# A fused graph network: the first attention chunk moved from the second norm into the first gate step

## What is computed

```python
x = _layernorm(x + _L0_gnn_ref(x, adj, ...))            # masked Gram matrix, rows normalised, times values
x = _layernorm(x + _L1_gnn_ref(x, adj, weight, bias))   # D^-1/2 A D^-1/2 x W + b
x = _layernorm(x + _L2_gnn_ref(x, adj, adj, ...))       # gated update, T = 3 steps
x = _layernorm(x + _L3_gnn_ref(x, adj, ...))            # attention over the neighbours, 8 heads

# inside _L2, three times (in_mat and out_mat are both adj)
a  = adj @ h
z  = sigmoid(a W3 + h U3 + b); r = sigmoid(a W4 + h U3 + b)
hv = tanh(a W5 + (r * h) U5 + b)
h  = (1 - z) * h + z * hv

# inside _L3
scores = q k^T / sqrt(32) + (1 - adj) * -1e9
out    = softmax(scores) v Wo + bo
```

## Time and profile before

| | |
|---|---|
| median of 3 runs | 2173.65 us (2171.86 to 2174.0) |
| the profiled execution | 2174.16 us, of which 2172.4 us are the span of the trace |
| TensorE | 2058.5 us busy (95%) |
| VectorE | 1573.2 us (72%) |
| ScalarE | 1251.9 us (58%) |
| GpSimd | 1016.2 us (47%) |
| mean granted TensorE clock | 0.986 of full speed |
| chain of work that ended last | PE 81%, DVE 8%, ACT 5%, issue 3%, POOL 2% |

### The profile page before, as it was taken

One profiled execution on the slowest core, in us unless ns is written; L12 is line 12 of the kernel. 1 busy time (PEld: TensorE's weight loads), 2 busy tenths in 40 slices (PEclk: granted clock), 3 DMA queues, 4 the chain that ended last, 5 costly groups with the idle time before them and its releaser, 6 DMA issues.

```text
span 2172.4 us, 34703 instructions
## 1 busy us (share of the span) xinstructions
PE 2058.5 (95%) x12342; PEld 1651.1 (76%) x12342; DVE 1573.2 (72%) x3441; ACT 1251.9 (58%) x2501; POOL 1016.2 (47%) x1138
## 2 busy tenths in 40 slices
PE   6789999999999999999999999999999999999976
PEld 4667787877878777787877878787787877778754
DVE  5566777687777777777777777767777776877756
ACT  3235656566564665646566565656656566564645
POOL 3113545445355554535545354554635454453545
PEclk8899999999999999999999999999999999999989
DMA  4002112030121203022120212212011120311222
GB/s 131 1 20 55 25 49 60 25 73 31 40 50 40 69 20 69 27 53 49 40 69 20 62 27 59 50 36 72 21 45 44 40 69 20 69 40 40 49 49 59
DMA packets 65632, 101.16 MB, mean 47 GB/s; under 512 B 11440, under 2 KB 31152, under 8 KB 65456
## 3 DMA queue, kind: packets, MB, share of 16 engines
q1 hardware_dynamic: 65456, 98.87, 17.9%
HBM read 23.34 MB, written 8.39 MB: 15 GB/s over the span
## 4 chain that ended last, share of the span: by engine, by line
PE 81%; DVE 8%; ACT 5%; issue 3%; POOL 2%; DMA 1%; SPq 1%; DVEq 0%; POOLq 0%; ACTq 0%
PE ps L958 17%; PE ps L960 16%; PE ps L959 16%; PE ps L980 12%; PE ps L1066 8%; PE ps L1050 4%; PE ps L1086 4%; DVE fa L937 1%; DVE fa L936 1%; ACT fa L430 1%; PE ps L1170 1%; PE ps L1353 1%; DVE fa L736 1%; POOL fa L328 1%; DVE fa L930 1%
## 5 line engine op out<-in xcount | busy, mean ns | idle before, releaser
L322 POOL TENSOR_TENSOR rsum<-esum,mhalf 128x2 f32<-128x2 f32 x256 | 211.1, 825 | 623.6 <-ACT fa L430 623.6
L736 DVE CUSTOM_DVE_ANT_0 fa<-ps,mask 128x512 f32<-128x512 f32 x512 | 332.3, 686 | 200.7 <-PE ps L1050 189.7
L328 POOL TENSOR_SCALAR fa<-fa,rsum 128x512 f32<-128x512 f32 x512 | 444.6, 881 | 53.0 <-POOL rsum L322 53.0
L430 ACT ACTIVATE fa<-fa,nmax 128x512 f32<-128x512 f32 x512 | 367.0, 725 | 54.6 <-DVE nmax L736 54.6
L425 ACT COPY pT<-ps 128x512 f32<-128x512 f32 x480 | 279.3, 585 | 194.4 <-PE ps L1066 194.3
L1066 PE MATMUL ps<-ident,fa 128*128 128x128 f32 x1920 | 285.9, 275 | 21.0 <-POOL fa L328 10.8
L1066 PEld LDWEIGHTS ps<-ident,fa 128*128 128x128 f32 x1920 | 227.7, 141 | 100.7 <-issue 26.0
L723 DVE TENSOR_TENSOR ra<-ps,ra 128x512 fp32r<-128x512 f32 x224 | 151.2, 687 | 186.7 <-ACT ra L554 93.5
L980 PE MATMUL ps<-adjT,ra 128*128 128x512 f32 x1024 | 260.6, 404 | 13.5 <-DVE ra L857 8.3
L980 PEld LDWEIGHTS ps<-adjT,ra 128*128 128x128 f32 x1024 | 191.9, 191 | 68.8 <-issue 9.0
L317 POOL TENSOR_TENSOR rstd<-veps,mhalf 128x2 f32<-128x2 f32 x128 | 98.2, 773 | 166.6 <-DVE veps L703 166.6
(11 more groups left out here) (195 smaller groups left out, 4738.8 us busy)
## 6 DMA issues: line engine op xcount, KB each, us to landing
ra<-ra SPq DMA_DIRECT2D x512, 128.0 KB, 2.4
fa<-in_x_T SPq DMA_DIRECT2D x17, 512.0 KB, 4.7
fa<-in_x SPq DMA_DIRECT2D x17, 512.0 KB, 3.9
out<-fa SPq DMA_DIRECT2D x15, 512.0 KB, 3.1
fa<-in_L_gnn_w_w SPq DMA_DIRECT2D x3, 512.0 KB, 8.6
adj_n<-in_adj SPq DMA_DIRECT2D x1, 1024.0 KB, 5.8
fa<-in_L_gnn_u_w SPq DMA_DIRECT2D x2, 256.0 KB, 9.2
out<-xn SPq DMA_DIRECT2D x2, 256.0 KB, 2.1
```

The lines of the kernel that those rows point to most:

```text
L322: nc.gpsimd.tensor_tensor(rsum[:, 2 * k:2 * k + 2], esum[:, 2 * k:2 * k + 2], mhalf[:, 4:6], ALU.pow).then_inc(rs_r, 1)
L328: nc.gpsimd.tensor_scalar(SC[:, g], SC[:, g], rsum[:, 2 * k + u:2 * k + u + 1], 1.0, ALU.mult, ALU.mult).then_inc(nrm, 1)
L430: nc.scalar.activation(SC[:, s % RING], SC[:, s % RING], ACT.Exp, bias=nmax[:, s:s + 1], scale=-1.0, accum_out=esum[:, s:s + 1]).then_inc( ...
L736: nc.vector.tensor_tensor_reduce(out=SC[:, s % RING], in0=ps[:, (4 if i is not None else lone_bank(k)) + u], in1=mask[:, 2 * (k % 8 // 4) ...
```

## The change

The first chunk's work leaves the second norm on all four engines:

- TensorE: score(1), back(0,0) and back(0,1) are no longer issued before the transposes of the norm. score(1) stands behind the gather of j = 0, score(2) behind `u3_of`, with back(0,0) just ahead of it. Behind w4's first half stand back(0,1), back(1,0) and score(3), behind w4's second half back(1,1), and back(2,0) stands between the two halves of w5.
- back(0,1) goes to PT_BANK like the others; the gather's wait for `pt_c` is gone.
- DVE: masked(0), masked(1) and masked(2) each move to the next place; masked(2) is now inside j = 0, behind `tile_lo`.
- ACT: exponentials(0) takes the place of exponentials(1) ahead of j = 0; exponentials(1), prob_copy(0,0), exponentials(2), prob_copy(0,1) and prob_copy(1,0) follow the copies of the gathered tiles; prob_copy(1,1) stands behind the two tanh.
- POOL: probabilities(0) comes behind `rstd_of(1, i)`.

Nothing is added or left out: the same instructions run in another order. The first pass (t is None) and the last (i is None) keep theirs.

```diff
--- before.py
+++ after.py
@@ -130,10 +130,7 @@
             return slice(2 * c, 2 * c + 2)
 
 
-
         def pt_bank(k, c):
-            if (k, c) == (0, 1):
-                return 0
             return 4 + c if k in (5, 9, 13) else PT_BANK
 
         adj_in = sem("adj_loaded"); w0_in = sem("layer_0_weights_loaded"); w2_in = sem("layer_2_weights_loaded")
@@ -361,12 +358,10 @@
                     rstd_of(0, i)
                     gp.wait_ge(x1_r, i + 1)
                     add_row(xg, b1row, xb_r)
-                if t is not None:
-                    probabilities(t, 0)
                 if i is not None:
                     rstd_of(1, i)
                 if t is not None:
-                    for k in range(1, 6):
+                    for k in range(6):
                         probabilities(t, k)
                 if o is not None:
                     rstd_of(3, o)
@@ -521,16 +516,12 @@
                 if i is not None:
                     tiles_hi(AB0, 0, t_ps, t_h)
                 if t is not None:
-                    exponentials(t, 0)
                     qk_hi(2)
-                    prob_copy(t, 0, 0)
                     qk_hi(3)
                 for c in range(2):
                     if i is not None:
                         act.wait_ge(x2_r, i * 2 + (c + 1))
                         copy(XNS[:, H, half(c)], xg[:, half(c)]).then_inc(xn_h, 1)
-                    if t is not None and c == 0:
-                        prob_copy(t, 0, 1)
                 if i is not None:
                     for d in range(DT):
                         act.wait_ge(hT_ps, i * 2 + (d + 1))
@@ -539,7 +530,7 @@
                         act.wait_ge(h_c, i * 2 + (d + 1))
                         copy(HTS[:, H, d], hT[:, d]).then_inc(hT_h, 1)
                 if t is not None:
-                    exponentials(t, 1)
+                    exponentials(t, 0)
 
                 for j in range(STEPS):
                     Z, D_, A, B_, C, E = [4 * j + k for k in range(2, 8)]
@@ -553,9 +544,11 @@
                             act.wait_ge(a_ps, m + (d + 1))
                             copy(AB0[:, H, d], ps[:, d]).then_inc(a_h, 1)
                     if t is not None and j == 0:
+                        exponentials(t, 1)
+                        prob_copy(t, 0, 0)
                         exponentials(t, 2)
+                        prob_copy(t, 0, 1)
                         prob_copy(t, 1, 0)
-                        prob_copy(t, 1, 1)
                     if t is not None and j == 2:
                         out_hi(t, 0)
                     if i is not None:
@@ -564,6 +557,8 @@
                             nc.scalar.activation(tr[:, d], ps[:, 2 + d], ACT.Tanh, bias=cols[:, BR, d:d + 1],
                                                  scale=0.5).then_inc(r_t, 1)
                     if t is not None:
+                        if j == 0:
+                            prob_copy(t, 1, 1)
                         prob_copy(t, Z, 0)
                         exponentials(t, D_ if j == 0 else A)
                         if j > 0:
@@ -864,8 +859,6 @@
                 if i is not None:
                     tile_lo(AB0, 0, 0, t_h, i * 2 + 1, t_l)
                     tile_lo(AB0, 0, 1, t_h, i * 2 + 2, t_l)
-                if t is not None:
-                    masked(0)
                 if i is not None:
                     dve.wait_ge(xb_r, i + 1)
                     sums_and_statistics(1, o1_ps, dinv, xg)
@@ -879,14 +872,14 @@
                     if t is not None and c == 0:
                         qk_lo(2)
                 if t is not None:
-                    masked(1)
+                    masked(0)
                     qk_lo(3)
                 if i is not None:
                     for d in range(DT):
                         dve.wait_ge(hT_h, i * 6 + (d + 1))
                         TT(HTS[:, L, d], hT[:, d], f32(HTS[:, H, d]), ALU.subtract).then_inc(hT_l, 1)
                 if t is not None:
-                    masked(2)
+                    masked(1)
                 if o is not None:
                     dve.wait_ge(x4a, o + 1)
                     x4_0, x4_1 = stats_of("o", X4, 3, 0), stats_of("o", X4, 3, 1)
@@ -902,6 +895,7 @@
                             tile_lo(AB0, 0, d, a_h, m + (d + 1), a_l)
                     if t is not None:
                         if j == 0:
+                            masked(2)
                             masked(3)
                         else:
                             masked(A)
@@ -1053,7 +1047,7 @@
                 def back(b, k, c):
                     if c == 0:
                         pe.wait_ge(nrm, b * TILES + (2 * k + 2))
-                    if k == 0:
+                    if k == 0 and c == 0:
                         pe.wait_ge(vv_r, b + 1)
                     elif pt_bank(k, c) == PT_BANK:
                         pe.wait_ge(pt_c, b * TILES + (2 * k + c - (2 if c == 0 and k - 1 in (5, 9, 13) else 0)))
@@ -1254,11 +1248,8 @@
                             if d == DT - 1 and s % 2 == 1:
                                 ins.then_inc(o1_ps, 1)
                 if t is not None:
-                    score(1)
                     qk_of(2)
-                    back(t, 0, 0)
                     qk_of(3)
-                    back(t, 0, 1)
                 if i is not None:
                     for s in range(NT):
                         if s % 2 == 0:
@@ -1286,15 +1277,14 @@
                     if t is not None and j == 1:
                         score(7)
                     if i is not None:
-                        if j == 0 and t is not None:
-                            pe.wait_ge(pt_c, t * TILES + 2)
                         gather(XNS, xn_l, m + 1, a_ps, qk_l if j == 0 and t is not None else None, (t or 0) * 4 + 3)
                     if t is not None:
-                        score(2 if j == 0 else A)
+                        score(1 if j == 0 else A)
                     if i is not None and j == 0:
                         u3_of(j)
                     if t is not None and j == 0:
-                        back(t, 1, 0)
+                        back(t, 0, 0)
+                        score(2)
                     for d in range(DT):
                         if i is not None:
                             pe.wait_ge(a_l, m + (d + 1))
@@ -1303,17 +1293,21 @@
                                 if d == DT - 1:
                                     ins.then_inc(r_ps, 1)
                         if t is not None and j == 0 and d == 0:
-                            back(t, 1, 1)
+                            back(t, 0, 1)
+                            back(t, 1, 0)
                             score(3)
                     if t is not None:
-                        back(t, Z, 0)
+                        back(t, 1 if j == 0 else Z, 1 if j == 0 else 0)
                         if j > 0:
                             score(B_)
                     if i is not None:
                         pe.wait_ge(a_l, m + 2)
-                        for d in range(DT):
+                    for d in range(DT):
+                        if i is not None:
                             for q in range(DT):
                                 block_of(0, W["w5"], AB0, q, d, d == 0, False)
+                        if t is not None and j == 0 and d == 0:
+                            back(t, Z, 0)
                     if t is not None:
                         back(t, Z, 1)
                         score(A if j == 0 else C)
```

## The result

The changed kernel takes 2224.56 us (median of 4 runs, 2221.69 to 2224.95), the kernel before 2172.76 beside it. The ratio of the times is 1.0236, 95% interval 1.0218 to 1.0254. The forecast was 2217 with a range from 2197 to 2230. Its two new waits are there, at the forecast sizes; what it counted only as a rival, a falling TensorE clock, came true in nine of the fifteen passes as well.

A forecast was written before the change was run, and what follows sets the result against it. TensorE, busy in 95% of the span, was taken as the bound. Per pass -0.45 + 1.35 - 0.12 + 1.15 + 0.95 = +2.88 us, times 15 passes +43 us, gave 2217 us, range 2197 to 2230.

The forecast's parts named there:

- two new waits: First gate step, TensorE: at back(1,0) for ACT's copy, 1.15 us; at back(3,0) for POOL's scaling, 0.95 us a pass.
- a falling TensorE clock: Rival, 20%: the clock falls in the norm, +0.80 us in half to all of the passes, 2223 to 2229 us.
- part 1: Second norm: with the attention work gone, the gather starts 0.45 us sooner; bounds 0 and 0.61.
- part 2: Gate step j = 0: the moved 1.35 us come back on TensorE, less 0.12 of idle time at w4's first half.
- part 3: Gate step j = 0: back(0,1) and back(1,0) share PT_BANK, so back(1,0) waits 1.15 us; ends 0.99 and 1.26.
- The walk: New order timed step by step from the gather: exponentials(2) delays ACT's copy, so back(1,0) waits 1.26 us.
- part 4: Gate step j = 0: exponentials(3) behind prob_copy(2,0) makes chunk 3 late, back(3,0) waits 0.95 us; bounds 0 and 1.1.
- The sum: All terms over a steady pass: +2.88 us, times 15 passes +43 us, giving 2217 us.
- the forecast's own: The case with both new waits and no fall of the clock: 50%, 2209 to 2223 us.

The follow-up runs named there:

- qkfirst: The kernel before, with qk_of(3) ahead of back(0,0) on TensorE and qk_hi(3) ahead of prob_copy(0,0) on ACT: 2170.3 us.
- qkstats: qkfirst with DVE's statistics of graph o moved behind the tile_lo of the first gate step: 2166.0 us.
- both: The changed kernel with back(0,1) in bank 0 again and exponentials(3) of the first gate step ahead of prob_copy(2,0) on ACT: 2191.2 us.
- all3: The changed kernel with the edits of bank0 and exp3 and the six matmuls of qk_of(3) repeated in the norm: 2185.3 us.
- bank0: The changed kernel with back(0,1) in bank 0 again, back(1,0) waiting only for the copy of back(0,0): 2196.4 us.
- exp3: The changed kernel with exponentials(3) of the first gate step ahead of prob_copy(2,0) on ACT: 2202.9 us.
- back20: The changed kernel with back(2,0) ahead of w5 again, right behind back(1,1): 2222.4 us.

## Why the prediction was right, and where it was short

**The norm (part 1).** Forecast: the gather 0.45 us sooner after DVE's first sum. DVE's sum and half of its variance in the changed kernel:

```profile
1244.05 0.88 DVE L712 SCALAR_TENSOR_TENSOR xn<-ps,dinv,xn 128x256 f32<-128x256 f32 x2 [1.38 <-PE ps L954]
...
1246.14 0.17 DVE L698 TENSOR_SCALAR veps<-mv 128x2 f32<-128x2 f32 x1
```

1250.76 - 1244.05 = 6.71 us against 7.34: 0.63 sooner, of which the gather gives back 0.08 by waiting for its second half (4.18 against 4.10). Net 0.55. The norm of the first pass (6.89 us) was a slow stand-in, because its clock had fallen (0.75 on average over 75 to 80 us): its last transposes took 1.11 us where those of the changed kernel took 0.66, and the gather came 0.77 us behind their start (77.81 to 78.58) and not 0.60 (1250.16 to 1250.76). That is 0.17 of the 0.18 us:

```profile
77.81 1.11 PE L1267 MATMUL ps<-ident,xn 128*128 128x128 f32 x4 [0.35 <-DVE xn L708]
```

Of the 0.63 some 0.3 is ACT's order, which qkfirst got by itself (0.33 a pass). Another 0.2 is visible in the variance: 0.17 us here, and in the kernel before

```profile
1090.65 0.40 DVE L703 TENSOR_SCALAR veps<-mv 128x2 f32<-128x2 f32 x1
```

while POOL scaled chunk 0 from 1090.33 on the earlier trace rows. It ended when POOL's first of two instructions did, at about 1091.0. The changed kernel has the like elsewhere: two of these instructions take 0.70 us from 1270.66, beside POOL's scaling from 1269.97 to 1271.33, and 0.29 in the kernel before (1113.46), where POOL was idle. That this is a collision of the two engines is read from the times alone; no run changed it by itself.

**The moved work (part 2).** 1.35 us came back into the gate step as forecast, and found nothing to hide in but the wait at w4. I priced that wait at 0.12 from start times. qkstats, which removes it, gained 0.27, so it was about twice as large; the changed kernel has no wait there. Parts 1 and 2 together are then -0.55 + 1.35 - 0.27 = +0.53 (forecast 0.78), between the 0.47 of "both" and the 0.63 of all3.

**The first wait (part 3).** Forecast 1.15 us from start to start; measured 1.60 - 0.44 = 1.16, and bank0 took 1.15 away. The walk found ACT behind exponentials(2): the trace has that copy right behind the exponential:

```profile
1260.70 0.70 ACT L425 ACTIVATE fa<-fa,nmax 128x512 f32<-128x512 f32 x1
...
1261.40 0.56 ACT L420 COPY pT<-ps 128x512 f32<-128x512 f32 x1
```

**The second wait (part 4).** Forecast 0.95; exp3 took 0.92 away (131.22 to 130.30). The lines that answer to the earlier trace rows are the copy for back(2,0), the first exponential of chunk 3, and POOL:

```profile
1266.97 0.59 ACT L420 COPY pT<-ps 128x512 f32<-128x512 f32 x1 [1.16 <-PE ps L1060]
1267.45 0.73 ACT L425 ACTIVATE fa<-fa,nmax 128x512 f32<-128x512 f32 x1
...
1269.97 1.36 POOL L325 TENSOR_SCALAR fa<-fa,rsum 128x512 f32<-128x512 f32 x2 [0.21 <-POOL rsum L319]
```

From 1267.45 to 1271.38 are 3.93 us, the very distance from the earlier trace rows.

**The sum.** Measured terms: -0.55 + 1.35 - 0.27 + 1.15 + 0.92 = 2.60 a pass, where the trace has 2.62 and I forecast 2.88. The terms that were off are the cover at w4 (0.12 for 0.27) and the norm's gain (0.45 for 0.55), both too small, 0.25 us together. The 0.27 is measured in another kernel, qkstats, and carried over.

**The clock.** I gave it 20% and a price of 0.80 us a pass in half to all of the passes, 2223 to 2229 us; it took 1.0 to 1.2 us in nine passes, and the total lies in that rival's range and not in the forecast's own (2209 to 2223). The likeliest case was mis-chosen: the idle time before the gather, which I had worked out as 2.2 us (the two waits in the trace are 1.71 and 0.35), lay between a case that kept its clock and one that lost it, and I took the sum without it. That 2217 is still within 8 us of the measured 2224.6 is in part luck: the sum was some 4 us too high for the waits and the work, and left out 10 us of clock.

The Trainium skill, "TensorE: Matmul & The Clock Gate", section "HAM oscillation — how this bites in real kernels", describes a loop whose every round loses the clock, after idle gaps that are longer than the waits here. Here the clock falls after shorter gaps, but in some rounds only: in 9, 2, 4, 9 and 8 of fifteen (changed, bank0, exp3, both, back20), kernels that differ by a microsecond or two a pass and have the same wait in the norm. So the length of the wait alone doesn't tell whether the clock falls. What decides it these runs leave open, and a range has to hold none and all.

## What to carry to other kernels

Work that fills a fixed chain of other engines is free only where it is. Before moving it out, price the chain without it (here the first pass showed 6.9 us and the changed kernel 6.7, against 7.3) and the place it goes to, which had 0.3 us to spare for 1.35. When one group of transposes moves in a hand-set order, walk both the bank it shares (group, copy, group: 1.43 us at least here) and the list of the engine that copies: each exponential or copy behind it moves with it, and a slack of 0.25 us is used up at once. And a wait that is lengthened on TensorE has a second price in its clock, which cheap filler work can buy back: it cost 0.1 to 0.16 us a pass here, against 1.0 to 1.2 for each fall. In the kernel before, the attention work in the norm was such filler.

## What the runs showed of the hardware

- Six matmuls whose result is thrown away made the kernel faster, 2212.6 against 2224.6 us, mostly by keeping TensorE's clock at 2.4 GHz in the nine passes that had lost it (some 10 us).
- With the same idle time in front, 1.45 us of work in 3.5, the granted clock fell in one pass (0.52 over the next 3.5 us) and stayed at 1.00 in another.
- A stretch of unchanged code at the end of the program varied from 90.5 to 98.2 us between kernels, as the low clock lay elsewhere in it.
